# Four attention layers on one core: row maxima carried into the stacked queries by DMA, turned scores half a step later

## The reference, cut to what matters

```python
# layers 0, 2 (self-attention), c (cross-attention inside layer 2) and 3, per head of width 8
scores = einsum('bhqd,bhkd->bhqk', q, k) * scale      # layer 2: plus causal and block masks
attn   = softmax(scores, axis=-1)                     # over the keys
out    = einsum('bhqk,bhkd->bqhd', attn, v)
# 0: x = norm(x + out @ wo + bo)      1: x = x + attention(rmsnorm(x)), 16 heads of 64
# 2: x = x + self(norm(x)); x = x + cross(norm(x), ctx); x = x + ff(norm(x))
# 3: x = norm(x + attention(x, ctx, ctx))
```

## Time and profile before

| | |
|---|---|
| median of 3 runs | 361.03 us (358.65 to 361.56) |
| the profiled execution | 359.1 us, span 357.3 us, so 1.8 us lie around the span |
| TensorE (PE) busy | 308.4 us, 86% of the span |
| VectorE (DVE), ScalarE (ACT), GpSimd (POOL) busy | 242.2, 212.7, 97.1 us |
| mean granted clock of TensorE | 0.981 |

### The profile page before, as it was taken

How to read it: one execution, slowest core, us unless ns; L and a number is a source line. 1 busy time by engine, 2 the same in 40 slices (tenths; PEclk the granted TensorE clock), 3 DMA queues, 4 the chain that set the end, 5 groups by cost and what they waited for, 6 DMA issues and landing times.

```text
span 357.3 us, 10164 instructions
## 1 busy us (share of the span) xinstructions
PE 308.4 (86%) x4069; PEld 215.2 (60%) x4069; DVE 242.2 (68%) x478; ACT 212.7 (60%) x459; POOL 97.1 (27%) x263
## 2 busy tenths in 40 slices
PE   2779999997999999988879999989886977998871
PEld 0434566775778778867655556556654765775550
DVE  7656478628987467667657456868876647667755
ACT  2247767757785785876745645646574553556560
POOL 8011734310310000101405534233342313423231
PEclk9969999999999999999999999999999999999898
DMA  6447740000000000001311322412332010011000
GB/s 215 146 123 209 253 186 5 2 0 2 2 2 2 0 2 0 2 2 46 84 50 37 85 69 68 121 31 74 91 90 61 3 47 24 24 46 38 25 17 29
DMA packets 26158, 20.65 MB, mean 58 GB/s; under 512 B 3192, under 2 KB 24960, under 8 KB 25856
## 3 DMA queue, kind: packets, MB, share of 16 engines
q1 hardware_dynamic: 24656, 18.44, 17.6%
q10 hardware_dynamic: 1456, 1.58, 1.4%
HBM read 6.63 MB, written 0.52 MB: 20 GB/s over the span
## 4 chain that ended last, share of the span: by engine, by line
PE 50%; DVE 16%; ACT 12%; issue 6%; SPq 5%; DMA 5%; POOL 4%; ACTq 1%; POOLq 0%
SPq L653 5%; PE psum L338 5%; ACT probs L822 5%; PE psum L780 4%; DMA qs<-part_q 4%; PE psum L311 4%; PE psum L695 4%; PE psum L746 4%; PE psum L721 3%; ACT probs L830 3%; PE psum L294 3%; PE psum L304 3%; DVE maxs L463 3%; PE psum L757 2%; PE psum L941 2%
## 5 line engine op out<-in xcount | busy, mean ns | idle before, releaser
L463 DVE TENSOR_REDUCE maxs<-psum 128x8 f32<-128x1024 f32 x64 | 77.8, 1215 | 48.3 <-PE psum L311 32.2
L389 ACT ACTIVATE probs<-psum 128x1024 f32<-128x1024 f32 x64 | 65.5, 1023 | 36.5 <-PE psum L304 36.3
L311 PE MATMUL psum<-ks,qs 64*128 64x128 bf16 x512 | 26.0, 221 | 14.8 <-DMA qs<-part_q 8.0
L338 PE MATMUL psum<-probs,vpad 128*32 128x128 f32 x1024 | 35.4, 280 | 0.0
L822 ACT ACTIVATE probs<-psum,maxs 128x128 f32<-128x128 f32 x128 | 34.8, 391 | 0.5 <-DVE maxs L871 0.5
L338 PEld LDWEIGHTS psum<-probs,vpad 128*32 128x32 f32 x1024 | 26.7, 111 | 12.2 <-ACT probs L389 6.4
L441 POOL CAST mp<-maxs 128x16 bf16<-128x16 f32 x32 | 6.9, 216 | 91.1 <-DVE maxs L463 90.6
L524 POOL TENSOR_SCALAR rstd<-stats 128x2 f32<-128x2 f32 (+1 forms) x19 | 4.2, 223 | 100.6 <-DVE stats L490 100.5
L311 PEld LDWEIGHTS psum<-ks,qs 64*128 64x128 bf16 x512 | 15.1, 95 | 24.6 <-issue 9.7
L881 DVE TENSOR_REDUCE mres<-probs 128x8 f32<-128x1024 f32 x16 | 19.4, 1215 | 12.3 <-ACT probs L822 12.3
L871 DVE TENSOR_REDUCE maxs<-psum 128x8 f32<-128x1024 f32 x16 | 19.5, 1220 | 11.7 <-PE psum L746 11.7
(11 more groups left out here) (154 smaller groups left out, 633.8 us busy)
## 6 DMA issues: line engine op xcount, KB each, us to landing
qs<-part_q SPq DMA_DIRECT2D x78, 64.0 KB, 2.0
ks<-part_k SPq DMA_DIRECT2D x30, 128.0 KB, 2.4
ks<-part_k SPq DMA_DIRECT2D x36, 64.0 KB, 2.0
wmat<-in_wmat SPq DMA_DIRECT2D x1, 1856.0 KB, 9.3
wmat<-in_wmat SPq DMA_DIRECT2D x1, 1024.0 KB, 5.1
qs<-part_q SPq DMA_DIRECT2D x6, 128.0 KB, 2.4
wrow<-in_wrow SPq DMA_DIRECT2D x1, 704.0 KB, 6.3
wmat<-in_wmat ACTq DMA_DIRECT2D x1, 512.0 KB, 8.2
```

The source lines that it names most:

```text
L311: s_mm = e.matmul(bank(2 * half + r)[:, bt(c)], qs[rows, i, bt(b)], ks[L.slot][rows, i, bt(b)], start=(c == 0), stop=L is not L2, skip_gro ...
L338: mm = e.matmul(o_bank(n)[rg(c), bt(half)], vpad[:, n % 2, 4 * half + c, G * a:G * a + G], pt, start=(a == 0), stop=(a == 1), skip_group_c ...
L389: e.activation(probs_of(n, half), bank(4, 2), ACT.Exp, scale=layer(n).scale)\
L463: e.tensor_reduce(maxs[:, n % 2, 8 * half:8 * half + 8], bank(2 * half, 2).rearrange("p (h k) -> p h k", k=P), AX.X, ALU.max, negate=True)\
```

## The change

1. The maxima go into slot 7 (`MAX_SLOT`) of the stacked queries, against ones in slot 7 of the keys, by one DMA per item (`max_rows`). The selector and the 512 matmuls of L304 are gone. The DMA is issued by ACT for items 0, 1, 2, 14, 16, 18, 20 and by SP for the other 25, at written places between the stacking DMAs. T waits for it (`rows0`, `rows1`).
2. Both halves of T of item s-2 now stand in step s. V is cut in two, `pe_V(n, 0)` at the end of step n+2 and `pe_V(n, 1)` in the first half of step n+3. back and norm move to the second half of n+3, onT to the first half of n+4. `end_of_even` on VectorE comes ahead of `dve_z`.
3. Slot rows are filled by DMA from small memset tiles (`ones`, `zeros`, both in `resid`): three DMAs at the start. The large memsets are gone, and GpSimd waits for `up` before it goes on. Slot 7 of `qs` has to be zero again for S of the next layer: `clear_q`, one DMA ahead of each of the 8 query stacks of layers c and 3, and two for layer 2.
4. Loads move between queues (masks, x, wrow, wcol, and the two large ones of `wmat`, to ACT; `v1` to SP). Value chunk 0 and the two `pe_v` groups of layer 0 move from before item 0 into step 0. The SP order in layers c and 3 puts the query stack ahead of the last key part, which GpSimd makes.

```diff
             if half == 0:
+                e.wait_ge(sem(f"rows{n % 2}"), 16 * (n // 2 + 1))
...
                 for c, r, rows, i in heads(mhalf):
-                    e.matmul(bank(4 + r)[:, bt(c)], ks[M.slot][rows, i, bt(b)], qs[rows, i, bt(b)],
-                             start=(c == 0), stop=False, skip_group_check=True)
+                    mm = e.matmul(bank(4 + r)[:, bt(c)], ks[M.slot][rows, i, bt(b)], qs[rows, i, bt(b)],
+                                  start=(c == 0), stop=M is not L2, skip_group_check=True)
...
-                e.wait_ge(sem("mT_read"), m + 1)
-                for i in range(4):
-                    for a in range(2):
-                        j = 2 * mhalf + a
-                        mm = e.matmul(bank(4 + a)[:, bt(i)], sel[rg(j), i, :], mrow[rg(j), m % 2, :],
...
-                pe_scores(e, n, 0, n2, 1)
+                pe_scores(e, n, 0, n2, 0)
                 ahead(s)
                 if n1 is not None:
                     pe_mT(e, n1)
+                if n4 is not None:
+                    pe_onT(e, n4)
                 even(s)
                 if n3 is not None:
-                    pe_back(e, n3)
+                    pe_V(e, n3, 1)
                 if n4 is not None:
                     pe_z(e, n4)
-                pe_scores(e, n, 1, n1, 0)
+                pe_scores(e, n, 1, n2, 1)
                 if n3 is not None:
-                    pe_onT(e, n3)
+                    pe_back(e, n3)
                 odd(s)
                 if n2 is not None:
-                    pe_V(e, n2)
+                    pe_V(e, n2, 0)
...
             e.copy(mrow[:, n % 2, :], m_turned(n)).then_inc(sem("mT_read"), 1)
+            if n in ROWS_ON_ACT:
+                max_rows(e, n)
...
+        ROWS_ON_ACT = (0, 1, 2, 14, 16, 18, 20)
+        def max_rows(e, n):
+            e.wait_ge(sem("mT_read"), n + 1)
+            e.dma_start(qs[MAX_SLOT::8, :, bt(n % B)], mrow[:, n % 2, :]).then_inc(sem(f"rows{n % 2}"), 16)
...
+        def clear_q(e, L, b0, nb):
+            e.wait_ge(sem("exp_done"), 2 * B * (L.at - 1) + 2 * (b0 + nb))
+            e.dma_start(qs[MAX_SLOT::8, :, toks(b0, nb)], kaug[:, 0:nb * P]).then_inc(sem(f"q_clear{b0}"), 16)
...
+            e.wait_ge(sem("fill"), 2)
+            e.dma_start(ks0[MAX_SLOT::8, :, :], ones.bitcast(BF16)).then_inc(sem("slots"), 16)
+            e.dma_start(qs[ROW_SLOT::8, :, :], ones.bitcast(BF16)).then_inc(sem("slots"), 16)
+            e.dma_start(qs[MAX_SLOT::8, :, :], zeros.bitcast(BF16)).then_inc(sem("slots"), 16)
...
-            stack_up(e, L3, "k", 0, 4)
-            stack_up(e, LC, "q", 4, 2)
-            stack_up(e, L3, "k", 4, 4)
-            stack_up(e, LC, "q", 6, 2)
...
+            for b0 in (0, 4):
+                max_rows(e, 17 + b0 // 2)
+                stack_dma(e, L3, "k", b0, 4, 0)
+                stack_dma(e, L3, "k", b0, 4, 1)
+                stack_up(e, LC, "q", 4 + b0 // 2, 2)
+                stack_dma(e, L3, "k", b0, 4, 2)
...
-            e.memset(qs[:, :, :].rearrange("p c t -> p (c t)").bitcast(F32), TWO_ONES).then_inc(sem("qs_one"), 1)
-            e.memset(wide_f32(ks0, 3), 0.0).then_inc(sem("ks0_zero"), 1)
+            e.wait_ge(sem("up"), 3)
```

More of the change, by code:

```diff
@@ L221, in data_of_S @@
             L, b = layer(n), n % B
-            return L.stacked("q", b) + L.stacked("k", b) + ([(sem("kaug_in"), 16)] if n == 0 else [])
+            ready = L.stacked("q", b) + L.stacked("k", b)
+            if n == 0:
+                ready += [(sem("kaug_in"), 16), (sem("slots"), 48)]
+            if n == B:
+                ready += [(sem("q_clear"), 32)]
+            if n >= 2 * B and b % 2 == 0:
+                ready += [(sem(f"q_clear{b}"), 16 * (n // B - 1))]
+            return ready
         FREED = {(0, 1): [(sem("kaug_out"), 1)],
@@ L434, in pool_split @@
             w, chain = n % 2, sem("split")
-            part = [mp[:, w, :].rearrange("p (j c) -> p j c", c=G)[:, :, 4 * k:4 * k + 4] for k in range(3)]
-            m = maxs[:, w, :].rearrange("p (j i) -> p j i", i=4)
-            r = mres[:, w, 0, :].rearrange("p (j i) -> p j i", i=4)
+            part = [mp[:, w, :].rearrange("p (r d c) -> p d r c", r=2, d=8)[:, k, :, :] for k in range(3)]
+            m = maxs[:, w, :].rearrange("p (r c) -> p r c", r=2)
+            r = mres[:, w, 0, :].rearrange("p (r c) -> p r c", r=2)
             e.wait_ge(sem("max_done"), 2 * n + 2)
@@ L654, in stack_dma, with stack_both @@
                      .then_inc(sem(f"{name}s{b0}"), 16)
+        def clear_q(e, L, b0, nb):
+            e.wait_ge(sem("exp_done"), 2 * B * (L.at - 1) + 2 * (b0 + nb))
+            e.dma_start(qs[MAX_SLOT::8, :, toks(b0, nb)], kaug[:, 0:nb * P]).then_inc(sem(f"q_clear{b0}"), 16)
         def stack_up(e, L, name, b0, nb):
+            if name == "q" and L.at >= 2:
+                clear_q(e, L, b0, nb)
             for p in range(3):
                 stack_dma(e, L, name, b0, nb, p)
+        def stack_both(e, L, b0, nb, ps):
+            for p in ps:
+                stack_dma(e, L, "k", b0, nb, p)
+                stack_dma(e, L, "q", b0, nb, p)
         def pe_v(e, L, g, to):
@@ L1157, in odd0 @@
             def odd0(s):
+                if s == 0:
+                    e.wait_ge(*L0.mm_done("q_rest", 2))
+                    pe_v(e, L0, 1, 6)
+                    e.wait_ge(sem("in_v1"), 16)
                 for i, c in enumerate(V1_ODD.get(s, ())):
@@ L1441, in _ @@
             e.memset(up[:, :, :], 0.0).then_inc(sem("up"), 1)
+            e.memset(ones, TWO_ONES).then_inc(sem("fill"), 1)
+            e.memset(zeros, 0.0).then_inc(sem("fill"), 1)
             u = sem("mask_split")
```

230 lines of the change are left out of this document (124 added, 106 removed).

## The result

The changed kernel takes **367.54 us** (median of 4, 365.67 to 369.39) where the kernel before takes 359.84 us beside it: a ratio of **1.021, 95% interval 1.014 to 1.029**. It is slower, and the prediction of 346.5 us (337 to 356) was wrong on both the size and the sign. Its profiled execution took 367.28 us, with a span of 365.0 us against 357.3. Some executions, of the kernel before too, are over 1.5% longer than the fastest of the same kernel: the medians here take in all executions, the ratios only the others, each against executions of the kernel before made beside them.

A forecast was written before the change was run, and what follows sets the result against it. The prediction took TensorE alone to bound layers 0 and 2, with other chains ending last at times elsewhere. Gains of 24.0 us less losses of 9.6 took 361.0 to 346.6, said as 346.5 us, range 337 to 356.

The forecast's parts named there:

- the first term: Removing L304's 512 matmuls across layers 0, 2, c and 3: 18.5 us gained, bounds 13 and 21.
- these two stages: Layers 0 and 2: TensorE alone sets the step, so 16 groups of 0.33 us gain 5.3 us in each.
- Layer c: All 16 removed L304 groups count in layer c, 5.3 us gained, if waits don't grow into the gap.
- Layer 3, 8 of 16 groups: In layer 3 a fixed-length chain ends last every second step, so 8 groups count: 2.6 us gained.
- Query stacks in layer c: The new SP order in layer c removes waits of S on query stacks: 3.5 us gained, bounds 0 and 4.5.
- The start: Without the fills key work begins 3 us earlier; 2 us gained up to S of item 1, bounds 0 and 4.
- V in halves: Cutting V adds 32 matmul group starts after a wait at 0.12 us each: 3 us lost, bounds 0 and 3.8.
- The seams: Losses at layer 0 to 1 (0.7 us), layer 1 to 2 (1.1) and the end (1.3).
- The clock, 1.5 us: TensorE's granted clock falls once more over a busy 3.4 us: 1.5 us lost, range 0 to 7.
- Rival C: The row DMA is late in every step, costing all 32 items: 373 us at a landing of 3.5; chance 0.05.
- Rival D: Clock low through much of layer 3, sign: below 1.00 between 290 and 330 us; 352 us, chance 0.1.
- A: Layers c and 3 give nothing, since stacks and VectorE end last: 356 to 358 us, chance 0.08.

The follow-up runs named there:

- the kernel without rows: The kernel after without the 32 row DMAs and T's waits on them, maxima left out of T: 359.0 us, ratio 0.996.
- row 8 on ScalarE: The kernel after with the row DMA of item 8 issued by ScalarE right behind its copy instead of by SP: 367.9 us, 1.015.
- memset start: The kernel after with slots filled by memsets, only the maxima slot's zeros by DMA, and start loads on their old queues: 367.8 us, 1.015.
- one pair of equal code: The mended one with ScalarE also issuing two stack DMAs of layer 3's queries, started with memsets (353.0 us) or slot DMAs (353.3 us); same code from item 10.
- the mended one: The kernel after with memset start, rows 0, 1, 8 to 31 on ScalarE behind osum, 2 to 7 and loads on SP, stacks and clears earlier: 358.1 us, 0.989.
- the fillings: The kernel after with eight extra matmuls ahead of S's query-stack waits of items 22, 24, 26, 28 and 30: 367.8 us, 1.018; also tried in combined runs.

## Why the prediction was wrong, point by point

The forecast missed by 21 us, and the kernel without rows splits the miss. Without its 2 us for the rows the forecast would have been 344.5 us, and that kernel takes 359.0: some 14.5 us are missing before any row is issued. The rows cost 8.5 us and not 2, which is the other 6.5. Of the 14.5 the first term is the largest part: 18.5 us were counted for L304, and taking it out of the kernel before gave 6. So two steps failed: busy TensorE was read as "TensorE alone", and a row was priced by its own landing. (The terms act on each other, so this is a split and no exact account.)

- **"In these two stages TensorE alone sets the step."** Right in layer 2: 0.66 us a step. Wrong in layer 0, 2.0 of 5.3 us. The busy row, 33.77 of 34.5 us, says that TensorE was busy, not how near the next engine was; with L304 gone, waits of 0.44 us on ScalarE's copies and up to 1.25 us on VectorE's norm appeared. I should have subtracted the time of the engine that ends next. In the kernel after even layer 2 gave 2.2 us of these 4.1: in the step from item 12 to 13 V's halves took 0.32 us and a wait on VectorE 0.29.
- **Layer c, "5.3 us, if the waits below don't grow into the gap".** They did: without L304 the stage took 37.1 for 36.9 us, in part by a clock that was low for 5 us of it. The step that failed is to count all 16 groups in a stretch with 7 us of idle TensorE.
- **Layer 3, 8 of 16 groups, 2.6 us.** Nothing, and the sign is wrong: 46.0 us for 44.0 with the work gone, part of it by the clock. Even the kernel without rows needs 45.3.
- **Query stacks in layer c, 3.5 us.** The mechanism held. With the rows out of the way the stage takes 33.7 for 36.9 us; the waits of items 16 and 20 are gone. In the kernel after a row stood ahead of the key parts, the wait of item 22 stayed (2.48, before 2.46), and little was seen of it.
- **"both can be issued before the first query part is ready, so I cost them at nothing here. If that cover is missing, each delays a stack by 0.64."** This is the failure that turned a small gain into a loss. The cover was missing at item 22 and in layer 3, and a row does more harm than its issue: the queue stands still until the row exists. I priced the 32 rows at 2 us by their landing (which was right, 1.8 us) and looked only at who waits for a row. The cost was on those queued behind it: 8.5 us, of which moving the issues brought back 7. The last line of the prediction came close, a row behind a part not yet made; what happened is the reverse, parts behind a row not yet made.
- **Rows on ScalarE** had no term at all. One that stood ahead of `onT` cost up to 0.77 us (item 15 to 16: 6.73 us in after, 5.96 with the issue behind `osum`). The Trainium skill, "DMA: Bandwidth & Descriptors", section "Issuing engines are not separate DMA queues", says that issuing from several engines saves only the time to initiate, "which is usually small relative to the DMA itself". Here the issue is 0.54 of a DMA of 1.8 us, and what stood behind it decided between a loss of 2% and none.
- **The start, 2 us gained.** 1.0 lost in the profiled execution, and 0.3 to 2.6 in three more kernels with the same start (table); S of item 1 stands at 27.56, beyond the 26 that was to say "nothing gained". I moved the key work forward rightly (VectorE's cast no longer waits), but took 3.2 us for DMAs that landed in 5.5 (stacks), 6.1 (mask row) and 8.4 to 9.5 us (the three slot DMAs of 256 KB) beside the loads. In the time of the kernel the start makes no difference that I could measure.
- **V in halves, 3 us.** Too small. In the steady step it is 0.32 us an item (V 0.14, z 0.10, the turn back 0.08 or 0.09), so an estimate of 5 us for the 16 items of layers 0 and 2 alone, and V's busy time rose from 35.4 to 43.1 us. That the first half also covers a wait was not seen.
- **The seams.** From 1 to 2: 1.1 predicted, 2.6 measured; all six stacks stood ahead of the row, not two thirds. The end: 1.3 predicted, 1.4 measured. From 0 to 1: 0.7 predicted, 0.8 measured from item 7 to 8.
- **The clock, 1.5 us.** Too small as a term, and perhaps more than a term: in two kernels (row 8 on ScalarE, memset start) a gain at one place was gone again behind stretches at the lower level. Up to 4.8 us in one pair of equal code.
- **Rival C** (row late in every step) was false: T waited for a row once. Rival D, by its own sign, was false too: from 290 to 330 us the clock of the kernel after is full, and it is low at the seam, at 274 us and from 335 us on (0.96, 0.97 and 0.76). It came true in kernels that were not predicted (0.91 without L304, 0.88 with row 8 on ScalarE). A was nearly true (layers c and 3 gave nothing). The time of the kernel without L304 alone, 355.2 us, is just under its 356 to 358. I gave A 0.08 although spoke for it, and had no rival in which those queued behind a row pay.

**Open:** what makes the clock fall. A wait alone does not: the kernel before waits 2.5 us once between 232 and 290 us at 1.00, and after waits 2.86 and 2.36 us between 290 and 332 us at 1.00. So whether a start 2 to 3.7 us shorter is lost to the clock by a mechanism or by chance is open too. Executions of one kernel spread by 2% (the mended one from 354.0 to 361.8 us in ten), and the fillings did not settle it. Nor was the new order of T and V tried without the cut, or L304 put back into the kernel after, so the 14.5 us are not parted further.

## What to carry to other kernels

A DMA issue that waits for data holds up everything behind it in its engine's program, so price it there: what stands behind it, when was that ready, who waits for it. Put it behind the last urgent instruction of the step, not straight behind its producer; here that one move was worth 2%, and from item 11 to 23 the rows then cost nothing. And before counting removed work as time, find the engine that ends next, since the gain stops there; test the pure removal first.

## What the runs showed of the hardware

- A DMA of 32 KB on 16 partitions costs SP 0.53 to 0.60 us and ScalarE 0.54 us of issue; on ScalarE the next copy started 0.94 us behind the one before it, against 0.16 us without an issue.
- A row DMA on the same queue behind a load of 1024 KB took 5.4 us to its consumer; the median row landed in 1.8 us.
- At the start a 64 KB stack DMA on ScalarE's queue lands in 2.1 us with the DMA engines 0.66 busy, and in 5.5 us with them 0.96 busy.
- In the one profiled execution without L304 the granted clock was 0.90 and 0.91, for 1.00, in the stretches in which TensorE then waited longer (11.3 us for stacks, 8.0 before). That the waits lowered it is not shown.
- A group of 32 matmuls in 32-column tiles took 1.01 us in one piece and 0.57 + 0.58 us in two.
